# A recommendation model's pairwise Gram on one core: one matmul per sample, transposed out of PSUM, with five transpose groups in every tile

## The chip, the cores and the metric

One core of one Trainium2 chip. The metric is the device time of the whole kernel in microseconds (us), as the median over several executions. Engines: PE is TensorE, PEld its weight loads, DVE is VectorE, ACT is ScalarE, POOL is GpSimd, SP is SyncE.

## The reference

A DLRM forward pass for 2048 samples in float32. 26 embedding rows of 64 numbers are fetched per sample, one dense row of 64 is added, all 27 x 26 / 2 = 351 inner products between the 27 rows are taken, and a four-layer network runs over everything.

```
h = relu(dense @ dw1 + db1);  dense_emb = relu(h @ dw2 + db2)
sparse_emb = emb_tables[f_ids, sparse_idx]                      # (2048, 26, 64)
emb = concatenate([dense_emb[:, None, :], sparse_emb], axis=1)  # (2048, 27, 64)
inter = einsum('bfd,bgd->bfg', emb, emb)                        # the Gram of each sample
pairs = inter[:, iu0, iu1]                                      # upper triangle, 351
z = relu(concatenate([emb.reshape(B, -1), pairs], axis=1) @ ow1 + ob1)
z = relu(z @ ow2 + ob2);  z = relu(z @ ow3 + ob3);  return z @ ow4 + ob4
```

## The kernel before, in words

The 2048 samples are worked in 16 tiles of 128, one sample per partition. There is no planner: each engine's program is written out by hand in the order in which it runs, and semaphores join them.

**POOL** (line 282) issues one indirect DMA per tile and embedding column, 128 rows of 256 bytes each: 16 x 26 less the 10 last columns of the tiles in `OWN`, so 406. The 10 missing columns are fetched row by row from the queues of SP and ACT (`fetch`). The destination `emb` is a ring of 4 tiles. At the start of tile t, from 2 on, POOL waits until tile t-2 has been transposed, its layer-1 output turned and its Gram done (lines 286 to 288).

**PE** transposes the gathered columns pair by pair (`transposes`, line 686): two columns of 64 are one block of 128, 13 blocks k per tile. They go in groups n, (0,4), (4,8), (8,12), (12,13), and a group waits for its own gathers. Two PSUM banks, `tr_ps[:, n % 2]`, take them in turn. Each group is then copied twice: `evac_features` makes `feat`, the stationary operand of layer 1 (line 759, 13 blocks), and `group_slots` makes `slots`, the same numbers with a sample's 27 rows side by side. ACT has groups 0 and 2, DVE groups 1 and 3.

**The Gram of tiles 0 to 14** (`gram`, line 725): four samples c and 32 slots are put together as one stationary operand of 64 x 128, and multiplied with the 4 x 27 columns of the same four samples. Of the 4 x 4 blocks of the result only the diagonal ones are wanted. A tile takes 32 such matmuls in two halves, into the four banks of `gram_ps`; two samples are kept in the two halves h of the partitions and go to different banks. `gram_copies` then picks the diagonal blocks (DVE rows 64 to 127, line 371; ACT rows 0 to 63, line 516) into `gram_c`, and `turn_gram` (line 378) transposes that 32 x 32-blockwise into `gram_b`. ACT's `pick_pairs` takes the 351 products from it (lines 522, 528), PE's `turn_pairs` (line 721) transposes them, DVE's `pairs_copy` (line 352) copies them, and `pairs1` (line 767) multiplies them with their part of layer 1. The second half of tile t-1's Gram is done after the first transposes of tile t.

**Layer 1** of a tile goes through `l1_ps`, is turned back (line 774, `h1_turned`), and layers 2 to 4 (`upper`, lines 791, 796, 800) run in batches of tiles, one stage at a time, at places between the tiles.

**The last tile**, 15, is its own case. It already has five transpose groups, `LAST_GROUPS` (`last_transposes`, line 704). Layer 1 is computed turned (line 854: 4 blocks m of 128 x 128, so that no turning back is needed). Its Gram is done in `last_gram` (line 802): samples c = 2, 3 two at a time (line 816, 64 x 64 stationary, 64 x 54 moving, into four borrowed places), whose diagonal blocks DVE and ACT move into `gram_ps` (`move_twos`, lines 404 and 584); samples c = 0, 1 one at a time (line 825, 64 x 32 stationary, 64 x 27 moving) straight into `gram_ps`. DVE's `turn_last_gram` (line 411) transposes out of PSUM. Then come ACT line 593 and DVE lines 416 and 423 (the picking), PE line 835, copies at 428 and 598, PE line 861, and layers 2 to 4 at lines 871, 879 and 885.

One float32 matmul stands in the trace as two MATMUL and two LDWEIGHTS records; a transpose as one of each.

## Time and profile before

| | us |
|---|---|
| median of 3 runs | 532.12 (531.58 to 532.66) |
| the profiled execution, its own time | 532.47 |
| its span, first to last instruction | 530.4 |
| POOL busy | 385.6 (73% of the span) |
| PE busy | 446.7 (84%) |
| PE weight loads | 237.3 (45%) |
| DVE busy | 155.2 (29%) |
| ACT busy | 150.1 (28%) |

The profiled execution spends 532.47 - 530.4 = 2.07 us outside its span. "Busy" is the time in which an engine had an instruction running; a busy share tells nothing of which engine sets the end. The mean granted clock of TensorE was 0.928 of full speed.

### The profile page before, as it was taken

How to read it: one execution, taken by the hardware profiler on the slowest of the kernel's cores; microseconds unless marked ns; L12 is line 12 of the kernel's file. 1: busy time of each engine (PE TensorE's matmuls, PEld its weight loads, DVE VectorE, ACT ScalarE, POOL GpSimd, SP SyncE). 2: the span in 40 equal slices, each digit the busy share in tenths (PEclk: the TensorE clock that was granted, in tenths of full speed). 3: DMA queues.
4: the chain of work that ended last, by engine and by line, in shares of the span. 5: the costliest groups of instructions: out<-in, count | busy, mean ns of one | idle time of the engine just before them, and what ended most of it. 6: DMA issues, size and time to landing. Idle time of an engine off the chain costs nothing.

```text
span 530.4 us, 8428 instructions
## 1 busy us (share of the span) xinstructions
PE 446.7 (84%) x2262; PEld 237.3 (45%) x2262; DVE 155.2 (29%) x297; ACT 150.1 (28%) x337; POOL 385.6 (73%) x410
## 2 busy tenths in 40 slices
PE   5958968687786979988696997988979899998998
PEld 1325424353442534444352443535334354535687
DVE  2311503323141321423332132331422323251342
ACT  2403213231241312423231241323223231422442
POOL 5777777777777777777777777777777777777740
PEclk9998989889797997999899797999897899999999
DMA  8321131111111111111111111111111111111110
GB/s 266 112 46 27 29 80 27 28 27 28 29 27 29 27 29 30 26 30 27 29 30 26 28 28 29 29 27 31 26 28 29 25 29 25 28 27 25 29 22 3
DMA packets 19429, 19.56 MB, mean 37 GB/s; under 512 B 9760, under 2 KB 10787, under 8 KB 19369
## 3 DMA queue, kind: packets, MB, share of 16 engines
q0 software_dynamic: 12992, 13.33, 11.5%
q1 hardware_dynamic: 5202, 5.26, 3.2%
q10 hardware_dynamic: 1188, 0.44, 0.4%
q8 instruction: 18, 0.29, 0.2%
q14 instruction: 29, 0.24, 0.1%
HBM read 18.99 MB, written 0.01 MB: 36 GB/s over the span
## 4 chain that ended last, share of the span: by engine, by line
POOL 53%; PE 23%; issue 19%; DMA 3%; DVE 1%; ACT 1%; POOLq 0%
POOL emb L292 52%; PE l_ps L759 7%; PE gram_ps L738 3%; PE l_ps L767 3%; DMA emb<-table_dram,rows 2%; PE tr_ps L791 1%; PE l_ps L854 1%; PE gram_ps L854 1%; POOL own L292 1%; PE tr_ps L700 1%; PE gram_ps L791 1%; PE l_ps L750 1%; PE l_ps L774 1%; ACT h L533 1%; DVE pairs L352 1%
## 5 line engine op out<-in xcount | busy, mean ns | idle before, releaser
L292 POOL DMA_INDIRECT emb<-table_dram,rows x396 | 375.9, 949 | 123.8 <-issue 119.4
L759 PE MATMUL l_ps<-w_sb,feat 128*128 128x512 f32 x390 | 202.4, 668 | 3.7 <-ACT feat L496 2.7
L759 PEld LDWEIGHTS l_ps<-w_sb,feat 128*128 128x128 f32 x390 | 80.1, 216 | 107.5 <-issue 100.0
L371 DVE COPY gram_c<-gram_ps 32x432 f32<-32x432 f32 x60 | 36.6, 610 | 150.8 <-PE gram_ps L738 150.4
L700 PE MATMUL tr_ps<-ident_sb,emb 128*128 128x128 f32 x194 | 35.7, 308 | 51.3 <-DMA emb<-table_dram,rows 50.3
L738 PEld LDWEIGHTS gram_ps<-slots 64*128 64x128 f32 x960 | 58.5, 195 | 15.8 <-issue 13.4
L738 PE MATMUL gram_ps<-slots 64*128 64x108 f32 x960 | 63.9, 285 | 1.3 <-DVE gram_c L371 1.3
L700 PEld LDWEIGHTS tr_ps<-ident_sb,emb 128*128 128x128 f32 x194 | 25.0, 154 | 82.3 <-issue 68.1
L516 ACT COPY gram_c<-gram_ps 32x432 f32<-32x432 f32 x60 | 30.5, 509 | 104.9 <-PE gram_ps L738 104.3
L338 DVE COPY feat<-tr_ps 128x512 f32<-128x512 f32 (+1 forms) x32 | 15.7, 492 | 141.1 <-PE tr_ps L700 141.0
L496 ACT COPY feat<-tr_ps 128x512 f32<-128x512 f32 (+1 forms) x32 | 18.5, 577 | 128.8 <-PE tr_ps L700 128.0
L767 PE MATMUL l_ps<-w1p_sb,pairs 118*128 118x512 f32 x90 | 42.6, 609 | 9.8 <-DVE pairs L352 9.8
L504 ACT COPY slots<-tr_ps 64x256 f32<-64x256 f32 (+1 forms) x128 | 50.4, 394 | 1.1
L347 DVE COPY slots<-tr_ps 64x256 f32<-64x256 f32 (+1 forms) x124 | 43.0, 347 | 1.3
L533 ACT ACTIVATE h<-l_ps 128x512 f32<-128x512 f32 x15 | 9.0, 597 | 68.8 <-PE l_ps L767 68.8
L767 PEld LDWEIGHTS l_ps<-w1p_sb,pairs 118*128 118x128 f32 x90 | 15.9, 189 | 27.8 <-issue 15.3
L378 DVE STREAM_TRANSPOSE gram_b<-gram_c 128x864 f32<-128x864 f32 x15 | 28.1, 1871 | 0.8
L791 PE MATMUL tr_ps<-h1t,w_sb 128*128 128x512 f32 x48 | 22.1, 603 | 0.0
L352 DVE COPY pairs<-tr_ps 118x384 f32<-118x384 f32 x15 | 8.4, 558 | 34.7 <-PE tr_ps L721 34.7
L750 PE MATMUL l_ps<-w1d_sb,dense_e 64*128 64x512 f32 x30 | 18.4, 698 | 0.0
L522 ACT COPY gram_b<-gram_b 128x169 f32<-128x169 f32 x15 | 5.0, 334 | 28.4 <-DVE gram_b L378 28.4
L791 PEld LDWEIGHTS tr_ps<-h1t,w_sb 128*128 128x128 f32 x48 | 8.7, 189 | 9.6 <-issue 9.1
(114 smaller groups left out, 219.9 us busy)
## 6 DMA issues: line engine op xcount, KB each, us to landing
own<-table_dram SPq DMA_DIRECT2D x896, 0.2 KB
emb<-table_dram,rows POOLq DMA_INDIRECT x396, 2.5
own<-table_dram ACTq DMA_DIRECT2D x384, 0.2 KB
w_sb<-ow_dram SPq DMA_DIRECT2D x3, 1024.0 KB, 8.9
w1p_sb<-ow_pairs_dram SPq DMA_DIRECT2D x1, 708.0 KB
w_sb<-ow_dram SPq DMA_DIRECT2D x1, 512.0 KB
w_sb<-ow_dram SPq DMA_DIRECT2D x1, 256.0 KB, 11.8
idx_raw<-idx_dram ACTq DMA_DIRECT2D x1, 208.0 KB, 6.6
```

The lines of the kernel that those rows point to most:

```text
L292: pool.indirect_dma_start(out=pair_of(t, c // 2)[:, c % 2 * D:(c % 2 + 1) * D], out_offset=None, in_=table, in_offset=bass.IndirectOffsetO ...
L347: last = nc.vector.tensor_copy(slots[t % 2][h * D:(h + 1) * D, :, :, base:base + b - a], src[:, h])
L371: last = nc.vector.tensor_copy(dst, src)
L378: nc.vector.transpose(gram_b[t % 2][:, 0:SLOTS, :], gram_c[:].rearrange("p i g -> p g i")).then_inc(gram_turned, 1)
L504: last = nc.scalar.copy(slots[t % 2][h * D:(h + 1) * D, :, :, base:base + b - a], src[:, h])
L516: last = nc.scalar.copy(dst, src)
L700: last = nc.tensor.transpose(tr_ps[:, n % 2, (k - a) * P:(k - a + 1) * P], pair_of(t, k), ident_sb[:])
L738: mm = nc.tensor.matmul(gram_ps[:, bank, r * GCOLS:(r + 1) * GCOLS], x.rearrange("p c f -> p (c f)"), x[:, :, 0:SLOTS], start=True, stop=True)
L750: nc.tensor.matmul(l1_ps[t % 2][:], dense_e[:, t * P:(t + 1) * P], w1d_sb[:], start=True, stop=False)
L759: nc.tensor.matmul(l1_ps[t % 2][:], feat[t % 2][:, n - 1, :], w1_sb[:, n - 1, :], start=False, stop=False)
L767: mm = nc.tensor.matmul(l1_ps[t % 2][:], pairs[t % 2][:, c, :], w1p_sb[:, c, :], start=False, stop=c == PC - 1)
L791: mm = nc.tensor.matmul(upper_ps(b, s)[:, 0:n], w2_sb[:, k, s * P:(s + 1) * P], h1t[b % 2][:, k, 0:n], start=(k == 0), stop=(k == M1 - 1))
```

## The change

Every tile gets the last tile's five groups, and their transposes go to four banks of `tr_ps` (the last tile keeps to banks 0, 1 and 3). `gram_ps` shrinks to two banks, one for each half h. The Gram of every tile, the last too, is 128 matmuls, one per sample, of 64 x 32 stationary and 64 x 27 moving, in one piece at the end of its tile, four samples c in the four column groups of the array. `gram_c`, `gram_copies`, `move_twos` and `turn_last_gram` go; `turn_gram` reads PSUM. In PE's order `turn_pairs(t-1)` moves ahead of the first five features of tile t, and two features are done between groups 2 and 3. DVE takes groups 1, 3 and 4, ACT groups 0 and 2. On ACT `pick_pairs(t-1)` moves ahead of `evac_features(t, 0)`.

```diff
-GROUPS = [(0, 4), (4, 8), (8, 12), (12, 13)]
+GROUPS = [(0, 4), (4, 8), (8, 10), (10, 12), (12, 13)]
-LAST_GROUPS = [(0, 4), (4, 8), (8, 10), (10, 12), (12, 13)]
...
-        tr_ps = psum("tr_ps", [P, 2, CHUNK])
-        gram_ps = psum("gram_ps", [P, SETS, CHUNK])
+        tr_ps = psum("tr_ps", [P, 4, CHUNK])
+        gram_ps = psum("gram_ps", [P, 2, CHUNK])
...
+        def bank(t, n):
+            return ((0, 1, 0, 1, 3) if t == LAST else (0, 1, 2, 3, 0))[n]
...
             def turn_gram(t):
-                dve.wait_ge(gram_copied, 4 * t + 4)
+                dve.wait_ge(gram_done, t + 1)
                 if t >= 2:
                     dve.wait_ge(pairs_picked, t - 1)
-                nc.vector.transpose(gram_b[t % 2][:, 0:SLOTS, :],
-                                    gram_c[:].rearrange("p i g -> p g i")).then_inc(gram_turned, 1)
+                src = gram_ps[:].rearrange("p h (j g) -> p g (h j)", g=QUAD)[:, 0:SLOTS, :]
+                nc.vector.transpose(gram_b[t % 2][:, 0:SLOTS, :], src).then_inc(gram_turned, 1)
...
             for t in range(LAST):
                 if t >= 1:
-                    gram_copies(t - 1, 0)
+                    turn_gram(t - 1)
                     if end_stage(t - 1) and end_stage(t - 1)[1] == 1:
                         hidden2(end_stage(t - 1)[0])
-                    gram_copies(t - 1, 1)
-                    turn_gram(t - 1)
                     pairs_copy(t - 1)
...
-                evac_features(t, 3)
-                group_slots(t, 3)
+                for n in (3, 4):
+                    evac_features(t, n)
+                    group_slots(t, n)
...
-            move_twos()
-            turn_last_gram()
+            turn_gram(LAST)
...
-            def gram(t, half):
-                if half == 0:
+            def gram(t):
+                if t == LAST:
+                    pe.wait_ge(slots_act, 2 * LAST + 4)
+                    pe.wait_ge(slots_dve, 3 * LAST + 3)
+                else:
                     pe.wait_ge(dense_slot, t + 1)
                     pe.wait_ge(slots_act, 2 * t + 2)
-                    pe.wait_ge(slots_dve, 2 * t + 2)
-                    if t == 14:
-                        pe.wait_ge(upper_out, out_count((3, 1)))
-                if 2 * t + half > 0:
-                    pe.wait_ge(gram_copied, 4 * t + 2 * half)
-                for j in range(half * HALF // 2, (half + 1) * HALF // 2):
-                    for h in range(2):
-                        x = slots[t % 2][h * D:(h + 1) * D, j]
-                        bank, r = 2 * h + j // SETS % 2, j % SETS
-                        mm = nc.tensor.matmul(gram_ps[:, bank, r * GCOLS:(r + 1) * GCOLS],
-                                              x.rearrange("p c f -> p (c f)"), x[:, :, 0:SLOTS],
-                                              start=True, stop=True)
+                    pe.wait_ge(slots_dve, 3 * t + 3)
+                if t >= 1:
+                    pe.wait_ge(gram_turned, t)
+                if t >= 14:
+                    pe.wait_ge(upper_out, out_count((3, 1) if t == 14 else (4, 2)))
+                for j in range(HALF):
+                    for c in range(SETS):
+                        for h in range(2):
+                            x = slots[t % 2][h * D:(h + 1) * D, j, c]
+                            mm = nc.tensor.matmul(gram_ps[c * QUAD:(c + 1) * QUAD, h, j * QUAD:j * QUAD + SLOTS],
+                                                  x, x[:, 0:SLOTS], start=True, stop=True)
                 mm.then_inc(gram_done, 1)
...
             for t in range(LAST):
                 transposes(t, 0)
                 if t >= 1:
-                    gram(t - 1, 1)
+                    turn_pairs(t - 1)
                 features1(t, 0, 5)
                 if t >= 1:
-                    turn_pairs(t - 1, 2 * t + 1)
                     pairs1(t - 1)
                 transposes(t, 1)
                 if t >= 1:
                     turn_hidden1(t - 1)
                 features1(t, 5, 9)
...
                 transposes(t, 2)
+                features1(t, 9, 11)
                 transposes(t, 3)
-                features1(t, 9, 14)
-                gram(t, 0)
+                transposes(t, 4)
+                features1(t, 11, 14)
+                gram(t)
                 if end_stage(t):
-                    upper(*end_stage(t), 2 * t + 2)
-            gram(14, 1)
-            upper(3, 3, 30)
+                    upper(*end_stage(t), 3 * t + 3)
             transposes(15, 0)
+            turn_pairs(14)
+            upper(3, 3, 45)
             last_features1(0, 5)
-            turn_pairs(14, 31)
             pairs1(14)
...
             last_features1(11, 12, (0, 1))
-            last_gram()
+            pe.wait_ge(dense_slot, LAST + 1)
+            gram(LAST)
             last_features1(11, 12, (2, 3))
             last_features1(12, 14)
             turn_last_pairs()
```

POOL's waits ask for the same as before, counted in the new units. The gathers, their number and their order stay.

## Rows read from the trace of the kernel before

**Rows 1.** The page: the chain that ended last by engine, and POOL's group of instructions

```profile
POOL 53%; PE 23%; issue 19%; DMA 3%; DVE 1%; ACT 1%; POOLq 0%
L292 POOL DMA_INDIRECT emb<-table_dram,rows x396 | 375.9, 949 | 123.8 <-issue 119.4
```

**Rows 2.** Timeline of POOL (start us, us): its first gather and four of tile 15's

```profile
3.69 1.08 POOL L292 DMA_INDIRECT emb<-table_dram,rows  x1 [3.23 <-DVE rows L315]
...
490.46 0.94 POOL L292 DMA_INDIRECT emb<-table_dram,rows  x1 [0.30 <-issue]
...
500.47 0.94 POOL L292 DMA_INDIRECT emb<-table_dram,rows  x1 [0.30 <-issue]
...
510.47 0.95 POOL L292 DMA_INDIRECT emb<-table_dram,rows  x1 [0.31 <-issue]
511.72 0.95 POOL L292 DMA_INDIRECT own<-table_dram,rows  x1 [0.30 <-issue]
```

**Rows 3.** The last gather's tile, `own`, from 505 us on: landing after issue

```profile
DMA to landing us min/median/max: 2.4/2.4/2.4
```

**Rows 4.** Timeline of PE: second half of tile 14's Gram, two groups of tile 15

```profile
492.10 2.04 PE L738 MATMUL gram_ps<-slots 64*128 64x108 f32 x32 [0.28 <-DVE gram_c L371]
...
494.59 0.66 PE L700 MATMUL tr_ps<-ident_sb,emb 128*128 128x128 f32 x4
...
504.11 0.60 PE L700 MATMUL tr_ps<-ident_sb,emb 128*128 128x128 f32 x4
```

**Rows 5.** Timeline of PE and DVE: tile 15 up to the turning of its Gram

```profile
513.07 0.38 PE L713 MATMUL tr_ps<-ident_sb,emb 128*128 128x128 f32 x2
...
514.38 0.30 PE L713 MATMUL tr_ps<-ident_sb,own 128*128 128x128 f32 x1
...
514.91 0.71 PE L854 MATMUL l_ps<-feat,w_sb 128*128 128x128 f32 x4
...
515.55 0.26 PE L816 MATMUL tr_ps<-slots 64*64 64x54 f32 x1
...
517.41 0.22 PE L816 MATMUL tr_ps<-slots 64*64 64x54 f32 x1
...
517.56 1.28 PE L825 MATMUL gram_ps<-slots 64*32 64x27 f32 x128
...
518.89 1.08 DVE L411 STREAM_TRANSPOSE gram_b<-gram_ps 128x864 f32<-128x864 f32 x1 [0.48 <-PE gram_ps L825]
```

**Rows 6.** Lines by form (busy us, mean ns): a record of the one-sample matmul

```profile
L825 PE MATMUL gram_ps<-slots 64*32 64x27 f32 x128 | 1.3, 190 | 0.0
```

**Rows 7.** Timeline after the last Gram: picking and turning its pairs

```profile
520.00 0.51 ACT L593 COPY pairs_b<-gram_b 128x182 f32<-128x182 f32 x1 [1.76 <-DVE gram_b L411]
...
521.10 0.38 PE L835 MATMUL tr_ps<-ident_sb,pairs_b 128*118 128x128 f32 x2
```

**Rows 8.** Timeline of PE: two waits for gathers, and ten layer-1 records twice

```profile
200.21 7.05 PE L759 MATMUL l_ps<-w_sb,feat 128*128 128x512 f32 x10
...
241.01 0.66 PE L700 MATMUL tr_ps<-ident_sb,emb 128*128 128x128 f32 x4 [1.22 <-DMA emb<-table_dram,rows]
241.60 2.04 PE L738 MATMUL gram_ps<-slots 64*128 64x108 f32 x32
...
367.55 0.66 PE L700 MATMUL tr_ps<-ident_sb,emb 128*128 128x128 f32 x4 [1.65 <-DMA emb<-table_dram,rows]
368.14 2.77 PE L738 MATMUL gram_ps<-slots 64*128 64x108 f32 x32
...
484.24 4.56 PE L759 MATMUL l_ps<-w_sb,feat 128*128 128x512 f32 x10 [0.57 <-ACT feat L496]
```

**Rows 9.** Stretches of 2 us: PE busy, its count, then granted clock, DMA share, GB/s

```profile
196.00:198.00 2.00, 0.00 (x0) 1.00 0.07 19
...
200.00:202.00 2.00, 2.00 (x4) 0.50 0.09 21
...
516.00:518.00 2.00, 2.00 (x107) 1.00 0.01 4
518.00:520.00 2.00, 2.00 (x109) 1.00 0.03 8
```

More of the change, by code:

```diff
@@ L125, in bass_dlrm_kernel @@
         ident_in = sem("ident_in")
-        w1_in = [sem(f"w1_in{n}") for n in range(NG)]
+        w1_in = [sem(f"w1_in{n}") for n in range(len(W1_PARTS))]
         w1d_in = sem("w1d_in")
@@ L130, in bass_dlrm_kernel @@
         gathered = [[sem(f"gathered{r}_{n}") for n in range(NG)] for r in range(RING)]
-        last_gathered = [sem(f"last_gathered{i}") for i in range(2)]
         out_stored = sem("out_stored")
@@ L294, in _ @@
                             in_offset=bass.IndirectOffsetOnAxis(ap=rows[:, t, c:c + 1], axis=0),
-                        ).then_inc(last_gathered[(c // 2 - a) // 2] if t == LAST and n == 2 else gathered[t % RING][n], 16)
+                        ).then_inc(gathered[t % RING][n], 16)
         @block.vector
@@ L395, in evac_half @@
             def evac_half(n):
-                a, b = LAST_GROUPS[n]
-                src = tr_ps[0:D, n % 2, 0:(b - a) * P].rearrange("p (k c) -> p k c", c=P)
+                a, b = GROUPS[n]
+                src = tr_ps[0:D, bank(LAST, n), 0:(b - a) * P].rearrange("p (k c) -> p k c", c=P)
                 nc.vector.tensor_copy(feat[LAST % 2][0:D, a:b, :], src).then_inc(feat_dve, 1)
-            def move_twos():
-                for part in range(2):
-                    dve.wait_ge(last_two, 2 * part + 2)
-                    for h in range(2):
-                        last = nc.vector.tensor_copy(*two_move(h, part, 3))
-                last.then_inc(last_moved, 1)
-            def turn_last_gram():
-                dve.wait_ge(gram_done, 2 * LAST + 1)
-                dve.wait_ge(last_moved, 2)
-                src = gram_ps[:, 0:2, :].rearrange("p k (j g) -> p g (k j)", g=QUAD)[:, 0:SLOTS, :]
-                nc.vector.transpose(gram_b[LAST % 2][:, 0:SLOTS, :], src).then_inc(gram_turned, 1)
             def pick_high_pairs():
@@ L498, in group_slots @@
             def group_slots(t, n):
[L499 removed]
+                a, b = GROUPS[n]
                 for half, base in ((0, a), (1, NP + a)):
[L501 removed]
+                    src = tr_ps[half * D:(half + 1) * D, bank(t, n), 0:(b - a) * P].rearrange(
                         "p (k c h j) -> p h j c k", k=b - a, h=2, j=HALF)
@@ L505, in group_slots @@
                 last.then_inc(slots_act, 1)
-            def gram_copies(t, half):
-                act.wait_ge(gram_done, 2 * t + half + 1)
-                if half == 0 and t >= 1:
-                    act.wait_ge(gram_turned, t)
-                for q in (0, 1):
-                    rows_q = slice(q * QUAD, (q + 1) * QUAD)
-                    src = gram_ps[rows_q, :, 0:SETS * GCOLS].rearrange(
-                        "p (h k) (r c g) -> p h k r c g", h=2, r=SETS, c=SETS)[:, :, :, :, q, :]
-                    dst = gram_c[rows_q].rearrange("p (h w k r) g -> p h w k r g", h=2, w=2, k=2)[:, :, half]
-                    last = nc.scalar.copy(dst, src)
-                last.then_inc(gram_copied, 1)
             def pick_pairs(t):
@@ L575, in evac_half @@
             def evac_half(n):
-                a, b = LAST_GROUPS[n]
-                src = tr_ps[D:P, n % 2, 0:(b - a) * P].rearrange("p (k c) -> p k c", c=P)
+                a, b = GROUPS[n]
+                src = tr_ps[D:P, bank(LAST, n), 0:(b - a) * P].rearrange("p (k c) -> p k c", c=P)
                 nc.scalar.copy(feat[LAST % 2][D:P, a:b, :], src).then_inc(feat_act, 1)
-            def move_twos():
-                for part in range(2):
-                    act.wait_ge(last_two, 2 * part + 2)
-                    for h in range(2):
-                        last = nc.scalar.copy(*two_move(h, part, 2))
-                last.then_inc(last_moved, 1)
             def pick_low_pairs():
@@ L662, in _ @@
             result(4)
-            move_twos()
             pick_low_pairs()
@@ L699, in transposes @@
                 for k in range(a, b):
[L700 removed]
+                    last = nc.tensor.transpose(tr_ps[:, bank(t, n), (k - a) * P:(k - a + 1) * P], pair_of(t, k),
                                                ident_sb[:])
                 last.then_inc(transposed, 1)
[L704 to L715 removed]
```

181 lines of the change are left out of this document (55 added, 126 removed).

## The prediction

> **What bounds the kernel now.** I read the page's chain first. 53% of the span is POOL's and 19% is "issue", and POOL's own group says what that issue is: 396 gathers of 949 ns with 123.8 us of idle time between them, 119.4 of it waiting for nothing the profile shows [rows 1]. So a gather costs 0.95 + 0.30 us. The timeline confirms the rhythm over the whole run: first gather at 3.69, last at 511.72 [rows 2], 405 steps, 1.2544 us each. POOL never stands still for another engine. PE is busy 84% of the span, but it is fed by this stream. Nothing that makes PE, DVE or ACT faster moves the last gather, and the change leaves number and order of the gathers alone.
>
> What can move is the part behind the last gather. It is issued at 511.72 [rows 2] and has landed 2.4 us later [rows 3], at 514.12; the span ends at 530.4. These 16.3 us are one chain of last-tile work. In the timeline [rows 5] the last transpose starts at 514.38, one feature's four records follow at 514.91, the Gram runs from 515.55, DVE turns it at 518.89, and picking, pairs, and layers 1 to 4 follow.
>
> How late PE is at each landing in tile 15 matters too: group 0 lands at 490.46 + 2.4 = 492.9 and PE takes it at 494.59, 1.7 us late; group 1 lands at 502.9, taken at 504.11, 1.2 late; group 3 lands at 512.9, taken at 513.07, 0.2 late; the last at 514.12, taken at 514.38, 0.26 late [rows 2 to 5]. PE catches up step by step and is nearly level at the end.
>
> **The change part by part.**
>
> *The last tile's Gram.* Before: 64 records of the two-sample form and 128 of the one-sample form. From the first record at 515.55 to the end of the block at 517.56 + 1.28 = 518.84 [rows 5] it takes 3.29 us. After: all 256 records have the one-sample form. The trace has this very form: 128 records in 1.28 us, one lasting 0.190 [rows 5, 6], so they start (1.28 - 0.19)/128 = 8.5 ns apart. 256 x 8.5 = 2.18, + 0.19 for the last = 2.37 us. Saved: 3.29 - 2.37 = 0.92 us. The row has samples c = 0, 1 in two column groups; the new stream uses four. The bounds for that unknown: if two more column groups run wholly beside the first two, 256 records take what 128 did, 1.28 us (saved 2.01); from the other side the nearest form is the two-sample one, which from 515.55 to 517.41 takes 1.86 us for 62 steps, 30 ns each [rows 5], or 7.7 + 0.2 = 7.9 us for 256 (lost 4.6). I take 8.5 ns, because it is the same shape, and keep both ends.
>
> A rule speaks against the change. TensorE: Matmul & The Clock Gate, in the Trainium skill, section "Wait — 56ns, not 53.3ns?", says start to start never drops below about 25 ns however small the moving operand is. By that page 256 records would be an estimated 6.4 us and the Gram would lose 3.1 us. The trace disagrees for this form: 8.5 ns [rows 5, 6].
>
> *The moves.* `move_twos` on DVE and ACT goes. It lay beside the one-sample matmuls: DVE waited 0.48 us for PE's L825 and for nothing else before it turned the Gram at 518.89 [rows 5]. Nothing gained. DVE's turning of the last tile already reads PSUM, 1.08 us [rows 5], and stays. Behind it ACT's pick ends at 520.00 + 0.51 = 520.51, PE's turning starts at 521.10 after its remaining features [rows 7]; both shift alike by the Gram's gain, and the 0.6 us between them stays, so all 0.92 us goes through to the end.
>
> *The Gram of tiles 0 to 14.* Before, two halves of 2.04 us [rows 4], 4.1 us of PE a tile, with copies by DVE and ACT between; after, 256 records, 2.37 us. PE gains 1.7 us a tile, DVE and ACT lose their `gram_c` copies, and DVE gains the small copies of group 3. All of this is hidden under 1.25 us x 26 = 32.6 us of gathers a tile: worth nothing in itself. POOL's waits at a tile's start ask for tile t-2's Gram and turned layer 1. These come earlier than before, since the second half of the Gram no longer stands ahead of them in PE's queue; even before they stopped no gather [rows 1]. If that cover went, a delay would move the whole stream by its own length.
>
> *PE's lateness.* The 2.04 us half [rows 4] no longer stands between the last landing of tile 14 and tile 15's group 0, and the other half and the splitting of group 2 take more out of the same stretch. So PE should wait at 492.9, at 502.9 and at 512.9 instead of coming late. From 512.9: transposes, one feature of eight records (about 0.9 us from 513.29 on), then the last transpose at 514.12 plus a few hundredths rather than 514.38. Bounds: 0.26 us gained, or nothing if DVE's or ACT's copies of group 3 are in the way. I take 0.2.
>
> *New waits.* Group 3 waits for `pairs_in` of the tile before, group 4 for ACT's slots of group 0, the last Gram for `upper_out` of stage (4, 2): each was made some microseconds earlier, and what is queued behind them on PE is work that waits for a gather anyway. Group 3's and 4's slot copies are behind each other on DVE and the Gram of tiles 0 to 14 waits for both; at most about 1 us a tile on PE, paid from the 1.7 it gained. The five semaphores on POOL's gathers cost no instruction. Taken as 0.
>
> *Sum.* 0.92 + 0.2 = 1.1 us. The profiled execution had 532.47 us (span 530.4, 2.07 around it), so it would be 531.4; it lies 0.35 above the median of the runs shown, 532.12. Against the median: **531.0 us**.
>
> **The rivals.**
>
> 1. *The clock falls in the tail (slower).* PE's granted clock was 0.50 at 200 to 202, after a stretch 196 to 198 in which PE did nothing at all; 1.00 is the 2.4 GHz level, 0.50 is 1.2 GHz [rows 9]. What it costs: the same ten layer-1 records took 7.05 us there and 4.56 at full clock [rows 8], 2.5 us. A wait of 1.22 us left the next Gram half at 2.04 us, one of 1.65 was followed by 2.77 [rows 8]. Before, PE was never idle that long in tile 15. After, a faster PE waits at 492.9, 502.9 and 512.9, by my count 1.0 to 1.4 us each. A fall at the first two would be made good by the waits that follow. It decides only if PE waits about 1.6 us before 512.9: then features and Gram behind the last landing run at the lower level. Price 2.5 us: 531.0 + 2.5 = 533.5. For it: the waits are near the bound. Against: PE reached tile 15's last groups level and not ahead, which leaves little to wait; and the clock held through 515 to 519 while small matmuls ran [rows 9].
> 2. *Four column groups overlap more (faster still).* Down to the 1.28 us bound: 2.01 + 0.2 = 2.2, 529.9; halfway 530.5. For it: the same column groups are independent. Against: nothing in the trace shows four at once.
> 3. *The tail doesn't notice.* If the last tile's Gram isn't what ends last but DVE's and ACT's slot copies in front of it, or the fixed steps behind it, the saving shrinks to below the 0.26 us at the transposes: 532.1. Against: PE runs without a pause from 514.38 to 518.84, and DVE waited for it.
> 4. *A floor for each matmul.* The four column groups share what feeds a row group, and each record costs the 30 ns of the two-sample form: 532.1 + 4.6 - 0.2 = 536.5. Against: the same shape at 8.5 ns. The page's 25 ns would belong to this case.
>
> **How the numbers follow.** Forecast 0.55; clock 0.18; more overlap 0.12; unnoticed 0.11; a floor 0.04. A measurement of this kernel can tell about 0.2%, 1.06 us, from no change, and the forecast's 1.1 lies just at that: with 0.2 us open at the transposes and some tenths of scatter (531.58 to 532.66 before), I give six tenths of it to faster, four to the same. Faster: 0.55 x 0.6 + 0.12 = 0.45. Same: 0.22 + 0.11 = 0.33. Slower: 0.18 + 0.04 = 0.22. The likeliest case's own range is 530.5 to 531.8. The range for 8 in 10 reaches from 530.2 (halfway into the overlap case) to 533.5 (the clock), leaving out the floor and the full overlap.
>
> **What the changed profile would show.** POOL: 406 gathers, first near 3.7, last at 511.7; if the last one moved, my first step is wrong. The last tile's 256 one-sample records in 2.2 to 2.4 us; 1.3 or 7.9 would be a rival's. DVE turning it near 517.8. The transposes of the last group at 514.1 to 514.2, with PE waiting for a gather ahead of it and of the groups before. Gram of other tiles 2.3 us, no copies of `gram_c`. A clock of 1.00 from 512 to the end; 0.50 there would be the first rival. The prediction is wrong if the time lies outside 530.2 to 533.5, or if it comes out near 531.0 with another Gram time than 2.4 us.

## The result, and the profile after it

The kernel after takes **545.97 us** (median of 6 runs, 540.19 to 549.20), the kernel before beside it 532.07 (6 runs). The ratio is **1.0185**, 95% interval 1.0156 to 1.0213: slower, by about 10 us at the ratio, where 531.0 was forecast. The ratio is taken over the three shorter executions, 540.19, 542.51 and 542.90 us; the other three, at 549 us, are slow ones and are left out of it, and with them the median lies 13.9 us above before. The profiled execution is the shortest of the six, 540.19 us with a span of 538.2, against 532.47 with 530.4 before. What follows explains these 7.8 us of span; the other 2 us of the ratio, and what made three executions 549 us long, have no profile and stay open.

The page of the kernel after: the span, the chain that ended last, POOL's group, and the queue that fetches PE's instructions.

```profile
span 538.2 us, 14216 instructions
...
q8 instruction: 41, 0.67, 0.5%
...
PE 66%; ACTq 9%; issue 9%; ACT 7%; POOL 4%; DVE 2%; DMA 2%
...
L277 POOL DMA_INDIRECT emb<-table_dram,rows x396 | 374.9, 947 | 124.8 <-issue 119.3
```

POOL's group is that of [rows 1]: the gathers didn't slow and hardly waited (2.4 us for PE in all), and the last one is issued at 511.76, where it was at 511.72 [rows 2]. Yet POOL's share of the chain has gone from 53% to 4% and PE's from 23% to 66%. PE is what the end waits for now. It was never as far from that as its 84% busy and the gathers' rhythm made it look. Its waits show where its room went.

Waits of PE by what ended them, kernel before (us in total, times, longest):

```profile
PE tr_ps L700 <- DMA emb<-table_dram,rows: 50.3, 25, 6.2
PE l_ps L767 <- DVE pairs L352: 9.8, 15, 0.7
...
PE l_ps L759 <- ACT feat L496: 2.7, 5, 0.8
...
PE gram_ps L738 <- DVE gram_c L371: 1.3, 3, 0.7
...
PE l_ps L759 <- DVE feat L338: 0.9, 1, 0.9
```

The same view, kernel after:

```profile
PE l_ps L682 <- ACT feat L452: 24.1, 15, 2.3
PE gram_ps L662 <- issue: 20.0, 24, 2.3
PE tr_ps L643 <- ACT pairs_b L472: 18.4, 13, 2.0
PE l_ps L682 <- DVE feat L323: 6.5, 16, 0.9
...
PE tr_ps L636 <- DMA emb<-table_dram,rows: 3.9, 2, 3.7
```

PE was busy 446.7 us before and 445.6 after, so the books are kept in waits. New ones: +21.4 us for ACT's feature copies, +20.0 within the Gram, +18.4 for ACT's picked pairs, +5.6 for DVE's copies; gone are 9.8 for DVE's pairs and 1.3 for `gram_c`. That is 54.3 us. PE paid 46.4 of it out of its waits for gathers (50.3 to 3.9). The remainder, 7.9, is about the span's 7.8, but it closes that well partly by chance: left out are 1.1 us less of busy time, 3.6 us of waits with "issue" as releaser ahead of transposes that the kernel before has and this one hasn't, and pauses too short for this view. The end of the timeline gives the 7.8 by itself, in two pieces. PE in tile 15, kernel after:

```profile
500.29 0.83 PE L636 MATMUL tr_ps<-ident_sb,emb 128*128 128x128 f32 x4
...
520.51 0.27 PE L636 MATMUL tr_ps<-ident_sb,own 128*128 128x128 f32 x1
...
521.66 1.50 PE L662 MATMUL gram_ps<-slots 64*32 64x27 f32 x155
525.50 1.05 PE L662 MATMUL gram_ps<-slots 64*32 64x27 f32 x101 [2.34 <-issue]
```

**Lateness**: group 0 is taken at 500.29, not 494.59, and the last transpose starts at 520.51, not 514.38 [rows 4, 5]: 6.13 us, of which 0.04 is POOL's. **The last Gram**: from 521.66 to 526.55 it is 4.9 us instead of 3.3 [rows 5], 2.34 of it a stop, and from the last transpose to the span's end it is 17.7 us instead of 16.0. Together 6.1 + 1.7 = 7.8.

**The Gram of the other tiles** is not the 2.4 us that was forecast either. One of them, 4.5 us long, kernel after:

```profile
240.72 1.32 PE L662 MATMUL gram_ps<-slots 64*32 64x27 f32 x99
242.19 1.11 PE L662 MATMUL gram_ps<-slots 64*32 64x27 f32 x60 [0.15 <-issue]
243.47 0.51 PE L662 MATMUL gram_ps<-slots 64*32 64x27 f32 x33 [0.17 <-issue]
244.67 0.56 PE L662 MATMUL gram_ps<-slots 64*32 64x27 f32 x36 [0.69 <-issue]
```

From the start of one record to the start of the next there are two kinds of long steps in tiles 0 to 14. Sixteen, of 0.3 to 1.9 us and 19.5 us together, are the stops that the next section explains. The other 73, of 0.13 to 0.38 us and 19.6 us together, keep time with POOL: 71 of them begin 0.3 to 0.5 or 1.1 to 1.2 us after the start of a gather, at most two to a gather. Behind the last gather there is none in the last tile's Gram. So a gather that runs beside such a stream holds it up once or twice, for about a quarter of a microsecond; why, no run shows.

### The profile page after: what moved, and what is told of

Read it like the earlier page. It is cut to its first block, busy times and chain, and to the rows that moved or that the text cites. A ratio compares the mean times of both kernels' runs of the same rounds, so it can differ in the third digit from the quotient of the medians.

```text
span 538.2 us, 14216 instructions
## 1 busy us (share of the span) xinstructions
PE 445.6 (83%) x5206; PEld 229.6 (43%) x5206; DVE 129.9 (24%) x308; ACT 105.6 (20%) x273; POOL 384.6 (71%) x410
## 3 DMA queue, kind: packets, MB, share of 16 engines
q1 hardware_dynamic: 5202, 5.26, 3.2%
## 4 chain that ended last, share of the span: by engine, by line
PE 66%; ACTq 9%; issue 9%; ACT 7%; POOL 4%; DVE 2%; DMA 2%
PE l_ps L682 28%; PE gram_ps L662 11%; ACTq L231 9%; PE l_ps L690 7%; PE tr_ps L716 5%; POOL emb L277 4%; PE l_ps L673 3%; ACT pairs_b L472 2%; PE tr_ps L721 2%; PE tr_ps L643 2%; ACT h L477 2%; DMA emb<-table_dram,rows 2%; PE tr_ps L636 1%; PE l_ps L751 1%; DVE feat L323 1%
## 5 line engine op out<-in xcount | busy, mean ns | idle before, releaser
L277 POOL DMA_INDIRECT emb<-table_dram,rows x396 | 374.9, 947 | 124.8 <-issue 119.3
L682 PE MATMUL l_ps<-w_sb,feat 128*128 128x512 f32 x390 | 200.0, 654 | 30.7 <-ACT feat L452 24.1
L682 PEld LDWEIGHTS l_ps<-w_sb,feat 128*128 128x128 f32 x390 | 74.6, 204 | 128.1 <-issue 79.8
L662 PE MATMUL gram_ps<-slots 64*32 64x27 f32 x4096 | 60.2, 201 | 24.5 <-issue 20.0
L323 DVE COPY feat<-tr_ps 128x512 f32<-128x512 f32 (+2 forms) x47 | 22.1, 470 | 218.8 <-PE tr_ps L636 218.3
L662 PEld LDWEIGHTS gram_ps<-slots 64*32 64x32 f32 x4096 | 49.4, 109 | 45.3 <-issue 43.5
L332 DVE COPY slots<-tr_ps 64x256 f32<-64x256 f32 (+2 forms) x184 | 62.7, 341 | 1.9
L460 ACT COPY slots<-tr_ps 64x256 f32<-64x256 f32 (+1 forms) x128 | 42.3, 330 | 1.1
L352 DVE STREAM_TRANSPOSE gram_b<-gram_ps 128x864 f32<-128x864 f32 x16 | 17.3, 1083 | 94.6 <-PE gram_ps L662 94.6
L452 ACT COPY feat<-tr_ps 128x512 f32<-128x512 f32 (+1 forms) x32 | 15.3, 477 | 99.6 <-issue 61.6
L716 PE MATMUL tr_ps<-h1t,w_sb 128*128 128x512 f32 x48 | 27.4, 724 | 1.6 <-issue 1.6
L643 PE MATMUL tr_ps<-ident_sb,pairs_b 128*118 128x128 f32 x45 | 9.5, 327 | 18.4 <-ACT pairs_b L472 18.4
L337 DVE COPY pairs<-tr_ps 118x384 f32<-118x384 f32 x15 | 8.4, 557 | 43.2 <-PE tr_ps L643 43.2
L643 PEld LDWEIGHTS tr_ps<-ident_sb,pairs_b 128*118 128x118 f32 x45 | 5.4, 154 | 21.9 <-ACT pairs_b L472 21.9
```

Source lines behind the costliest of these rows:

```text
L277: pool.indirect_dma_start(out=pair_of(t, c // 2)[:, c % 2 * D:(c % 2 + 1) * D], out_offset=None, in_=table, in_offset=bass.IndirectOffsetO ...
L323: nc.vector.tensor_copy(feat[t % 2][:, a:b, :], src).then_inc(feat_dve, 1)
L332: last = nc.vector.tensor_copy(slots[t % 2][h * D:(h + 1) * D, :, :, base:base + b - a], src[:, h])
L460: last = nc.scalar.copy(slots[t % 2][h * D:(h + 1) * D, :, :, base:base + b - a], src[:, h])
L643: mm = nc.tensor.transpose(turned(c), pairs_b[t % 2][:, c * PR:(c + 1) * PR], ident_sb[:])
L662: mm = nc.tensor.matmul(gram_ps[c * QUAD:(c + 1) * QUAD, h, j * QUAD:j * QUAD + SLOTS], x, x[:, 0:SLOTS], start=True, stop=True)
```

## The experiments

A run is read by three numbers: the ratio to the kernel before run beside it, how long after the issue of the last gather the last transpose starts ("lateness", 2.66 us before, of which 2.4 is the landing), and how long the tail behind that transpose is (16.0 before). Seven runs fell on two chips on which the kernel before itself takes 869 to 871 us (called the slow chips here); they are told with the others, and compared with their own before only.

### The last tile's Gram alone

`b_last1` is the kernel before with the last tile's Gram as 256 one-sample matmuls; `b_last1_gap` cuts them in two blocks of 128 around five layer-1 features (20 records).

```diff
-                for part in range(2):
...
-                    for c in range(2):
+                    for c in range(SETS):
...
-            move_twos()
```
```diff
-            last_gram()
+            last_gram(0)
             last_features1(11, 12, (2, 3))
             last_features1(12, 14)
+            last_gram(1)
```

> The kernel before with one edit: the last tile's Gram is 256 one-sample records, move_twos is gone; the other 15 tiles are untouched. Supply theory (PE takes the one-sample records faster than its instruction stream is refilled): the 256 records show at least one gap of 1 to 2.5 us that the page calls issue, the block takes 4 to 5 us in place of 3.29, and the kernel is 0.5 to 1.7 us slower than before. Order theory (the loss comes from where the change puts its waits in PE's order, the one-sample records run at 8.5 ns throughout): block 2.4 us, kernel 0.9 us faster. Clock theory: as order theory, with granted clock 1.00 here.

> As b_last1, but the last tile's Gram is split: 128 records, then the 20 layer-1 records of 0.11 us that used to follow, then the other 128. Supply theory: the pause lets the stream be refilled, so the gap inside the records shrinks by about the 2.2 us that stand between, to under 0.5 us. Any theory in which the gap belongs to the records themselves (PSUM writes, four column groups) keeps it. The turning of the Gram now comes after those features, so about 1 us more than b_last1 would be without a gap: 532 to 533 us.

> The kernel of b_last1 again, on a chip where the kernel before takes 532 us (if it is one): only the last tile's Gram is 256 one-sample records. Supply theory, with what the trace of b_last1 showed (a gap of 2.3 us inside the records, and the features behind it slower for a while): block 4.7 to 5.4 us in place of 3.29, 1.5 to 3 us slower than before, 533.6 to 535.1. My prediction's sum: 0.9 us faster, 531.2.

`b_last1`: 0.9987 (0.9954 to 1.0019) on a slow chip. `b_last1_2`, the same kernel on a chip where before takes 532: **1.0037** (1.0021 to 1.0052), a loss where my forecast has its whole gain. PE's timeline of `b_last1_2` (the longest of its nine executions):

```profile
515.98 0.71 PE L835 MATMUL l_ps<-feat,w_sb 128*128 128x128 f32 x4
516.62 1.96 PE L806 MATMUL gram_ps<-slots 64*32 64x27 f32 x211
520.67 0.58 PE L806 MATMUL gram_ps<-slots 64*32 64x27 f32 x45 [2.08 <-issue]
521.19 0.87 PE L835 MATMUL gram_ps<-feat,w_sb 128*128 128x128 f32 x4
521.85 1.06 PE L835 MATMUL l_ps<-feat,w_sb 128*128 128x128 f32 x4
```

And of `b_last1_gap` (a single execution on a slow chip, 876.08 us, span 874.1):

```profile
857.79 1.28 PE L806 MATMUL gram_ps<-slots 64*32 64x27 f32 x128
859.00 0.71 PE L836 MATMUL gram_ps<-feat,w_sb 128*128 128x128 f32 x4
...
861.43 1.46 PE L806 MATMUL gram_ps<-slots 64*32 64x27 f32 x128
```

211 records run in 1.96 us, 8.4 ns apart less the last one's 0.19: the step I had from 128 records [rows 5, 6] holds, and with four column groups. Then PE stands for 2.08 us and waits for nothing that the profile shows, and after that its clock is low: layer-1 records come at 1.06 us for four, 0.61 at full clock. In the cut version the same 256 matmuls on the same operands, banks and column groups take 1.28 and 1.46 us, and their longest step is 0.15 us. So the stop belongs to how many instructions follow each other without a break, not to the matmul's form. Whether cutting pays is not shown: the single execution is no measure against 871 us, though from the last transpose to the end it takes 17.5 us where `b_last1` takes 19.0.

What runs dry is PE's instructions. The page says only "issue", but the trace says more when PE's records (matmuls, weight loads and semaphores) are numbered in their order. The instruction queue moves packets of 16 KiB: 41 for 10520 records in the kernel after, 18 for 4651 in the kernel before and for 4777 in `b_last1_2`, so one packet for about 256 records. The thirteen traces of this document's table and of `a_halves_2` have 82 steps of over 0.7 us inside a Gram. All 82 come at the same place of a 256, at record 193 or 194 counted modulo 256, none anywhere else, and each ends 1.2 to 1.6 us after a packet has landed. The kernel before has none. `b_last1_gap` passes the very record, number 4546, before which `b_last1_2` stands, and there is its 0.15 us. In the kernel after the last Gram crosses such a border after 27 records without a step and stops at the next one, after 27 + 128 = 155; in `b_last1_2` they lie after 83 and 211. Two packets never start less than 3.2 us apart in any trace, while a block of 256 records, half of them matmuls, is used up in 1.1 us at 8.5 ns a matmul. An estimate from this, if 3.2 us is the least that the queue can do: a long stream of such matmuls is supplied at no better than 3.2 us / 128 = 25 ns each.

The Trainium skill, Runtime: NRT & Kernel Launch, section "Instruction fetch mechanics", has instructions fetched in blocks of 16 KiB (the packets agree) and crossing from one block to the next "mostly hidden". In the Gram of the kernel before that is so. In the new Gram these runs disagree: up to 2.8 us, 2.08 here and 2.34 in the kernel after.

### The order on PE, and the Gram in halves

`a_order` is the kernel after with two orders on PE put back: `turn_pairs` behind the first five features, and features 9 to 13 together behind group 4. `a_halves` also cuts the Gram of tiles 0 to 14 into two blocks of 128, the second behind the next tile's first transposes. `a_turn` moves `turn_pairs` alone.

```diff
                 transposes(t, 0)
-                turn_pairs(t - 1)
                 features1(t, 0, 5)
+                turn_pairs(t - 1)
...
                 transposes(t, 2)
-                features1(t, 9, 11)
                 transposes(t, 3)
                 transposes(t, 4)
-                features1(t, 11, 14)
+                features1(t, 9, 14)
```

> The changed kernel with PE's order of before put back: turn_pairs(t-1) behind the first five features of tile t, and features 9 to 13 together behind group 4. The Gram stays 256 one-sample records. Order theory: the waits for ACT's pick (18.4 us in the changed kernel) and for ACT's group 2 (24.1 us) go, PE meets the gathers again, and the time falls to 531 to 533 us. Supply theory: the Gram's gaps stay, and the time falls by only part, to 535 to 541 us.

> The kernel of a_order once more, because the chip of the first four runs took 871 us for the kernel before and is no measure of a run at 532 us. PE's order of before is put back (turn_pairs behind five features, features 9 to 13 together behind group 4); the Gram stays 256 one-sample records. Order theory: 531 to 533 us where before takes 532. Supply theory: the Gram's gaps of 1 to 2.3 us stay, one or two a tile, and the time is 535 to 541 us.

> As a_order, and in addition the Gram of tiles 0 to 14 in two halves of 128 records, the second behind the first transposes of the next tile, as the kernel before had it. Supply theory: each half is one refill's worth of instructions, gaps shrink, and it is 1 to 5 us faster than a_order; only the last tile keeps its gap. Order theory: the same as a_order within 1 us.

> The kernel of a_halves again: a_order with the Gram of tiles 0 to 14 in two halves of 128 records. Supply theory: a refill still falls due about every 128 records of Gram, wherever the halves stand, so a stall of up to 2.3 us stays wherever one falls into a half, and the gain over a_order (539.1) is small, 0 to 3 us: 536 to 539. If instead the length of the unbroken stream is what matters, the gaps go in tiles 0 to 14, PE meets the gathers again, and it is 534 to 535 (the last tile's gap alone is left).

> The changed kernel with one line moved back: turn_pairs(t-1) behind the first five features. It takes away the 18.4 us that PE waited for ACT's pick in 13 tiles, and keeps features 9 and 10 between groups 2 and 3. If that wait is the larger part of what a_order gained (7 us against the changed kernel's median, 3 against its fast runs), this one is at 539 to 541; if the features are, it stays at 541 to 546.

On a slow chip `a_order` came to 1.0368 and `a_halves` to 1.0472. On one where before takes 532, `a_order_2` is **1.0123** (1.0099 to 1.0147), `a_turn` 1.0164 (1.0146 to 1.0182), against 1.0185 after. `a_turn` takes away the 18.4 us of waiting for the pairs, but PE then waits 30.8 us for ACT's copies instead of 24.1. With both orders back the copies cost 10.6 and the gathers 28.7; the lateness is still 8.1.

`a_halves_2` is a miss: 1.0206 (1.0151 to 1.0261), not better than `a_order_2`, and its four executions scatter from 539.58 to 549.33. PE in the profiled one:

```profile
461.90 1.78 PE L664 MATMUL gram_ps<-slots 64*32 64x27 f32 x124
464.08 0.25 PE L664 MATMUL gram_ps<-slots 64*32 64x27 f32 x4 [0.40 <-issue]
464.26 1.12 PE L676 MATMUL l_ps<-w1d_sb,dense_e 64*128 64x512 f32 x2
467.18 6.40 PE L685 MATMUL l_ps<-w_sb,feat 128*128 128x512 f32 x8 [1.80 <-ACT feat L452]
```

The stops in the Gram have shrunk (4.6 us over the run, from 11.7), but the first group's features wait for ACT, 41.4 us in all. The change put ACT's `pick_pairs` of the old tile ahead of its copy of the new tile's group 0, and the pick waits for the whole Gram. And behind that wait the eight records take 6.40 us at a granted clock of 0.50, where 3.70 is usual. Halving the Gram without moving the pick back gains nothing: the ratio is above `a_order_2`'s, and the profiled executions of the two have the same span, 537.5.

### The row fetches on ACT

Group 2 has two pairs now, and ACT's first 16 own-row fetches stand ahead of its copy of them. `a_fetch` puts both batches behind that copy; `a_both` is `a_order` and `a_fetch`.

```diff
-                fetch_some(2 * t)
                 evac_features(t, 2)
                 group_slots(t, 2)
+                fetch_some(2 * t)
                 fetch_some(2 * t + 1)
```

> The changed kernel with one edit on ACT: both batches of 16 row fetches come after the copies of group 2, where one came before them. In the changed kernel PE waited 24.1 us for ACT's copy of group 2, up to 2.3 us a tile, most of it in the tiles in which ACT still fetches. Order theory: these waits fall to about 0.5 us a tile and the kernel gains 1 to 4 us on the changed one. Supply theory: the gain is absorbed before tile 12, where the fetches end, so nothing: 540 to 546.

> a_order and a_fetch together: the changed kernel with PE's old order and with ACT's row fetches behind its group 2 copies. a_order alone measured 1.0123 and a_fetch alone 1.0117 times before. If both took away the same lateness of PE, this is again 1.011 to 1.012 (538 to 539); if they are two things, 1.005 to 1.008 (535 to 536.5). Order theory alone would have 1.000. The last tile's gap, worth 1.0037 by b_last1_2, stays in any case.

ACT's timeline of the kernel after, with the batch ahead of the copy:

```profile
228.13 5.23 ACTq L231 DMA_DIRECT2D own<-table_dram  x16
233.41 0.37 ACT L452 COPY feat<-tr_ps 128x256 f32<-128x256 f32 x1 [5.46 <-issue]
```

and PE's, group 2's transposes and the features behind them:

```profile
231.56 0.38 PE L636 MATMUL tr_ps<-ident_sb,emb 128*128 128x128 f32 x2
233.83 3.14 PE L682 MATMUL l_ps<-w_sb,feat 128*128 128x512 f32 x4 [1.88 <-ACT feat L452]
```

ACT does nothing but issue fetches for 5.46 us ahead of the copy, and PE stands idle for 1.88 us until the copy is there. In `a_fetch` (**1.0117**, 1.0099 to 1.0134) this wait falls from 24.1 to 6.9 us. `a_both` is 1.0113 (1.0091 to 1.0135): the two repairs don't add up at the median, though the lateness falls from 8.1 and 8.4 to 4.7 us.

### The new Gram in the old kernel

`b_gram` is the kernel before with the new Gram, in halves and at the old places, for tiles 0 to 14, and DVE turning it out of PSUM; four groups, all orders and the last tile are left as they were. `b_gram_last` is `b_gram` with `b_last1`'s last tile.

```diff
                 for j in range(half * HALF // 2, (half + 1) * HALF // 2):
-                    for h in range(2):
-                        x = slots[t % 2][h * D:(h + 1) * D, j]
...
+                    for c in range(SETS):
+                        for h in range(2):
+                            x = slots[t % 2][h * D:(h + 1) * D, j, c]
...
-                    gram_copies(t - 1, 0)
...
-                    gram_copies(t - 1, 1)
```

> The kernel before with the new Gram in tiles 0 to 14 alone: 256 one-sample records a tile in two halves at the old places, DVE turns them straight out of PSUM, no gram_c copies. Groups, PE's order, ACT's and DVE's lists and the last tile stay as before. Supply theory: two or three refills fall due a tile in place of one, some inside the records, each up to 2.3 us; PE comes later to tile 15's last group than 514.4, and the kernel is 1 to 5 us slower, 533 to 537. Order theory: PE's work a tile is no longer than before and nothing else moved, so 532 within 1 us.

> b_gram and b_last1 together: the whole new Gram in the old schedule with four groups. What it lacks of the changed kernel is the five groups, the four transpose banks, the order and the one-piece Gram. Supply theory: the sum of both, 1.0037 plus b_gram's, 1.006 to 1.013. If it comes near 1.0185, the schedule of the change cost nothing of its own; what is left between it and a_both is the groups and the one-piece Gram.

`b_gram` is **1.0011** (0.9998 to 1.0025): no difference that can be told. Its stops in the Gram are 3.9 us, its waits for gathers 45.8. `b_gram_last` is **1.0052** (1.0031 to 1.0073), about the sum of `b_gram` and `b_last1_2` (1.0011 and 1.0037); lateness 2.73, tail 18.8. So the Gram itself is 0.5%, most of it in the last tile, and over 1% of the 1.85 lies in the schedule: the orders, the five groups and the Gram in one piece. That halves and old places make the new Gram harmless in tiles 0 to 14 doesn't mean that it runs at 8.5 ns: `b_gram` has only 2 steps at a block's border there that are long (1.06 and 1.45 us), but 71 pauses beside gathers, 19.5 us.

### The pick, and every order put back

`a_pick` moves ACT's pick back behind its copies of group 0, on top of `a_both`; `a_old` cuts the Gram in halves on top of that, so that only five groups with their banks and copies differ from `b_gram_last`; `a_pick1` moves the pick alone in the kernel after.

```diff
-                    pick_pairs(t - 1)
                 evac_features(t, 0)
                 group_slots(t, 0)
                 if t >= 1:
+                    pick_pairs(t - 1)
                     hidden1(t - 1)
```

> a_both, and ScalarE picks the pairs of the tile before behind its two copies of the new tile's first group, as the kernel before does. If the pick ahead of these copies is what is left, the ratio to before falls from 1.0113 to about 1.006 and the wait of TensorE's layer-1 matmuls for ScalarE's feature copy falls from 9.7 us to under 5. If the five groups or the unbroken Gram are, it stays within 1.009 to 1.013, and with the pick later the wait of the first transposes' successors for the pairs may grow by as much as the other falls.

> a_pick, and the Gram of tiles 0 to 14 is cut in two halves of 128 matmuls, the second behind the first transposes of the next tile. Every order is then that of the kernel before; five groups instead of four, with four banks, are all that differs from b_gram_last (1.0052). If the unbroken Gram (its waits for instructions) and the pick are the rest, this gives 1.004 to 1.007. If the five groups cost by themselves, it stays at 1.009 or more.

> The kernel after, with ScalarE's pick of the pairs behind its copies of the first group, and nothing else moved. TensorE turns the pairs right behind the first transposes here, so a later pick makes that wait longer: by the theory that this order and the pick belong together the ratio rises above after's 1.0185, to 1.020 to 1.030. If the pick ahead of the copies is the main loss by itself, it falls to 1.010 to 1.014.

> The kernel of a_pick again, meant for a chip on which the kernel before takes 532 us. If the pick of the pairs ahead of ScalarE's copies is the rest, the ratio falls from the 1.0113 of a_both to about 1.006; if the five groups or the unbroken Gram are, it stays within 1.009 to 1.013.

> The kernel of a_old again. On the slow chip it came to 0.998 of before, against 1.014 for a_pick: there the unbroken Gram was the rest and the five groups cost nothing. If that holds here, the ratio is 1.004 to 1.007, as b_gram_last's (1.0052), which has the same last tile; if the five groups cost by themselves here, it stays at 1.009 or more.

> The kernel of a_pick1 again. On the slow chip it came to 1.11, far worse than any other. If the later pick only makes the wait for it longer where TensorE turns the pairs right behind the first transposes, the ratio here is above after's 1.0185, 1.020 to 1.030; if that was a matter of the slow chip alone, it is 1.010 to 1.018.

On a slow chip: 1.0140, 0.9979 (0.9949 to 1.0009) and 1.1105. On one where before takes 532.15: `a_pick_2` 1.0090 (1.0062 to 1.0117), `a_old_2` **1.0074** (1.0058 to 1.0090), `a_pick1_2` **1.1374** (1.1335 to 1.1413), 605 us. The last is the most telling of all. PE in `a_pick1_2`:

```profile
262.87 0.60 PE L636 MATMUL tr_ps<-ident_sb,emb 128*128 128x128 f32 x4
266.97 0.90 PE L643 MATMUL tr_ps<-ident_sb,pairs_b 128*118 128x128 f32 x3 [3.51 <-ACT pairs_b L472]
267.80 2.07 PE L673 MATMUL l_ps<-w1d_sb,dense_e 64*128 64x512 f32 x2
269.80 5.00 PE L682 MATMUL l_ps<-w_sb,feat 128*128 128x512 f32 x8
```

PE has nothing between group 0's transposes and the pairs; ACT copies group 0 before it picks; so PE stands 3.51 us, once in each tile (51.3 us in all), and the low clock behind the stop (granted 0.50 from 266 to 272) makes the two dense records 2.07 and the eight features 5.00 instead of 1.12 and 3.70. PE comes so late that POOL has to wait too. The same move in `a_pick_2`, where PE has five features to do in the meantime, took PE's waits for ACT's feature copies from the 9.7 us of `a_both` to 1.5. The pick ahead of the copy and `turn_pairs` ahead of the features are one decision in two queues; taking back ACT's half alone costs 12%, taking back PE's half alone (`a_turn`) gains nothing that can be told.

`a_old_2` shows what halves do for the gathers:

```profile
488.04 1.80 PE L664 MATMUL gram_ps<-slots 64*32 64x27 f32 x128
489.78 1.13 PE L724 MATMUL tr_ps<-h,w_sb 128*128 128x256 f32 x4
492.35 0.66 PE L636 MATMUL tr_ps<-ident_sb,emb 128*128 128x128 f32 x4 [1.44 <-DMA emb<-table_dram,rows]
492.93 1.82 PE L664 MATMUL gram_ps<-slots 64*32 64x27 f32 x128
```

PE does the first half, waits 1.44 us for tile 15's first group, and is on time for it. The halves take 1.80 and 1.82 us here at full granted clock, where the same 128 took 1.28 in the last tile of `b_last1_gap`: these are the pauses beside gathers. In `a_pick_2`, with one block ahead of these transposes, PE's last wait for a gather is at 419.48; from there on it is behind.

| kernel | ratio | last gather | lateness | tail | span | waits for gathers |
|---|---|---|---|---|---|---|
| before | 1 | 511.72 | 2.66 | 16.0 | 530.4 | 50.3 |
| b_gram | 1.0011 | 510.52 | 2.66 | 16.5 | 529.7 | 45.8 |
| b_last1_2 | 1.0037 | 511.57 | 3.87 | 19.1 | 534.5 | 56.2 |
| b_gram_last | 1.0052 | 510.76 | 2.73 | 18.8 | 532.3 | 41.2 |
| a_old_2 | 1.0074 | 511.05 | 2.81 | 18.8 | 532.7 | 43.2 |
| a_pick_2 | 1.0090 | 510.66 | 5.53 | 17.2 | 533.4 | 29.1 |
| a_both | 1.0113 | 510.64 | 4.71 | 18.6 | 534.0 | 19.4 |
| a_fetch | 1.0117 | 510.65 | 8.41 | 18.7 | 537.8 | 20.2 |
| a_order_2 | 1.0123 | 510.48 | 8.08 | 18.9 | 537.5 | 28.7 |
| a_turn | 1.0164 | 511.18 | 7.86 | 18.7 | 537.7 | 5.7 |
| after | 1.0185 | 511.76 | 8.75 | 17.7 | 538.2 | 3.9 |
| a_pick1_2 | 1.1374 | 565.32 | 15.74 | 19.0 | 600.1 | 4.1 |

(us; the profiled execution of each, which is the shortest of its runs in `after`, `a_both`, `a_old_2` and `b_gram`, and the longest in `b_last1_2`. In `b_last1_2` the last transpose waited 0.44 us for its landing. In `a_pick1_2` POOL itself was held up: 177.9 us of idle time between its gathers, 124.8 in the kernel after.)

With all orders back the lateness is back as well. Five groups against four is 1.0074 against 1.0052 with intervals that overlap: these runs don't tell it from nothing. `a_both` to `a_old_2` go down step by step, but neighbours overlap too; only the whole path is shown, and which of pick and halves gave how much of the last 0.4% stays open. No version beat the kernel before by more than its interval.

The tails of 18.6 and more against 17.2 and 17.7 have one cause. Stretches of 2 us in `a_both` (PE busy, its count, granted clock, DMA share, GB/s):

```profile
518.00:520.00 2.00, 0.00 (x1) 1.00 0.00 0
520.00:522.00 2.00, 1.95 (x105) 0.56 0.04 8
522.00:524.00 2.00, 2.00 (x12) 0.58 0.00 0
```

and in `a_pick_2`:

```profile
520.00:522.00 2.00, 1.25 (x103) 1.00 0.04 8
522.00:524.00 2.00, 2.00 (x20) 1.00 0.00 0
```

Behind the stop of the last Gram (2.04 and 1.91 us) the clock fell to the lower level in the first and held in the second; 12 records against 20 in the stretch from 522. It fell so in all the kernels of the table with the one-sample last tile but `a_pick_2` and the kernel after, in the profiled execution of each. How long PE stood doesn't decide it: the clock fell behind 1.86 us in `a_old_2` and held behind 2.34 in the kernel after. With the stop itself taken off, the tails are 15.3 and 15.4 us where it held and 16.3 to 17.0 where it fell, so the price is 1.0 to 1.7 us.

## Why the prediction was wrong

- **"256 x 8.5 = 2.18, + 0.19 for the last = 2.37 us", so 0.92 us saved**: the failed step for the last tile. The 8.5 ns is right where no gather runs. The stream of 128 records it came from [rows 5] could not show the second border of an instruction block in one stream, which came after 155 records here: the last Gram took 4.9 us, a loss of 1.6 where 0.92 was to be gained. `b_last1_2` prices it at 1.0037, some 2 us. The bound above (7.9 us) held; the value was taken at the row, though the new stream was twice as long as any that the row had.
- **"PE gains 1.7 us a tile ... worth nothing in itself"**: the first half failed. PE's 960 old records took 63.9 us and 1.3 of waits in 15 tiles, 4.3 a tile. After, the 4096 records have 60.2 busy and 20.0 of stops; less the last tile's 2.55 and 2.34 that is 75.3, 5.0 a tile. PE lost 0.7 us a tile. The step that failed is "after, 256 records, 2.37 us": 15 x 2.37 = 35.6 us, and nearly all of the 39.7 us above it are the 19.5 us of stops at the borders of instruction blocks and the 19.6 us of pauses beside gathers. The 8.5 ns came from the one Gram behind the last gather. The second half failed because the cover was counted over the whole run: POOL's 32.6 us a tile against PE's work, 50.3 us of room in all. It was not in tile 15's reach, since before PE last waited for a gather at 461.58.
- **"New waits ... Taken as 0"**: the largest failure. I listed waits on semaphores that the diff adds and none that its new order makes. `turn_pairs` right behind group 0 waits for ACT's pick, 18.4 us; two features behind the short group 2 wait for a copy that stands behind 16 fetches, 24.1 us; the row of [rows 8] with its 0.57 us wait for ACT `feat` had pointed there. "at most about 1 us a tile on PE, paid from the 1.7 it gained" was 2.8 us a tile for these two less the 0.8 they replace, and nothing was gained to pay it from.
- **"PE's lateness", 0.2 gained**: the sign was wrong. PE was to wait at 492.9, 502.9 and 512.9; it never waited for a gather in the last tiles, and was 6.1 us later than before. This one term is four fifths of the 7.8.
- **The sum of POOL** was right: 396 gathers of 947 ns, 119.3 us of issue, last one 0.04 us later. *The moves* were right at nothing, as far as `b_gram` shows: without the `gram_c` copies it is 1.0011.
- **The rivals.** The clock was a right mechanism at a wrong place: in the last tile it fell, where it did, behind the stop inside the Gram, not behind a wait for a gather, and costs 1.0 to 1.7 us where 2.5 were put; in the profiled execution of the kernel after it held at 1.00. More overlap of four column groups (1.28 us for 256) didn't happen. A floor of 30 ns for each record is refuted by 211 records in 1.96 us, and with it, for this form, the 25 ns of the Trainium skill's page TensorE: Matmul & The Clock Gate, section "Wait — 56ns, not 53.3ns?". No rival had the instructions running dry, or an engine's order as what it waits for.

## What to carry to other kernels

A duration per record is good for a stream as long as the one that it was read from, and for what ran beside it: when a change doubles the number of instructions in one unbroken block, bound the block by a stop of its own, and put other work in the middle. That makes a stop rarer and not impossible: 128, 20 others, 128 ran with a longest step of 0.15 us, but a half of 128 in `b_gram` still met one of 1.25. Keep books of a nearly full engine by tile: 50 us of waits over a run are no cover at the end if the last of them is 70 us before it. And when two queues hand a result to and fro, an order moved in one is a wait in the other: list for each moved call what the other engine has ahead of the thing it waits for, and look at both halves of the pair before one is moved.

## What the runs showed of the hardware

Four column groups and two row groups of 64x32 operands take a new matmul each 8.5 ns for up to 211 records, as long as no gather runs. Then PE stood, for 1.8 to 2.6 us in the last tile of each of the eleven kernels that have the 256 in one piece, always at the border of a 256-record block of instructions. Beside gathers the stream also paused once or twice a gather, for 0.1 to 0.4 us. That a sequence of small matmuls costs more in its supply than in its arithmetic was not in my count at all.

On two other chips the kernel before took 869 to 871 us. ACT's timeline there (`b_last1`) has batches of own-row fetches of two kinds:

```profile
419.76 5.26 ACTq L246 DMA_DIRECT2D own<-table_dram  x16
426.45 0.47 ACTq L246 DMA_DIRECT2D own<-table_dram  x1
427.02 29.65 ACTq L246 DMA_DIRECT2D own<-table_dram  x15
```

Sixteen in 5.26 us, as elsewhere, and then 15 in 29.65, where `b_last1_2` has 4.68 for 15 on its chip:

```profile
264.80 4.68 ACTq L246 DMA_DIRECT2D own<-table_dram  x15
```

It is not the fetches alone. PE crawled in the same stretch, where nothing that the trace shows was in its way:

```profile
442.69 0.37 PE L697 MATMUL tr_ps<-ident_sb,emb 128*128 128x128 f32 x1 [2.41 <-issue]
445.49 0.37 PE L697 MATMUL tr_ps<-ident_sb,emb 128*128 128x128 f32 x1 [2.43 <-issue]
```

POOL's gathers kept their 1.25 us meanwhile, but over the run POOL waited 314.8 us for PE, which is most of the difference to 532. What slowed the other engines was not found. Ratios from the slow chips and the others differ by up to 3%, with both signs (`a_order` 1.0368 and 1.0123, `a_old` 0.9979 and 1.0074), so a gain of 1 or 2% found on the one kind does not carry over to the other.
